# Attention and the experts' entry in one block: normalization, turns and gate logits of seven batches inside the attention's last steps

## What is computed

```python
# L0 attention: 16 heads of 64, relative bias
scores = einsum("bqhd,bkhd->bhqk", q, k) / 8 + bias
x = layernorm(x + softmax(scores) @ v @ Wo)
# L0 ffn: 8 experts, each token takes the best two, one after the other
gate_logits = x @ gate_W + gate_b
gate_weights = softmax(gate_logits)
topk_vals, topk_idx = top_k(gate_weights, 2)
out_1 = expert[idx_1](x);  out_2 = expert[idx_2](x + 0.5 * out_1)
x = layernorm(layer_norm(x + w_1 * out_1 + w_2 * out_2, gamma, beta))
```

## Time and profile before

| what | us |
|---|---|
| median of three runs | 1908.12 |
| the three runs | 1909.07, 1902.9, 1908.12 |
| the profiled execution | 1909.93 |
| its span, first to last instruction | 1907.8 |
| from the span's start to the end of the attention's last addition | 804.6 |
| from there to the gates' exponential | 26.4 |

### The profile page before, as it was taken

How to read it: one execution, slowest core, us unless ns; L and a number is a source line. 1 busy time by engine, 2 the same in 40 slices (tenths; PEclk the granted TensorE clock), 3 DMA queues, 4 the chain that set the end, 5 groups by cost and what they waited for, 6 DMA issues and landing times. The chain is left out here.

```text
span 1907.8 us, 39508 instructions
## 1 busy us (share of the span) xinstructions
PE 1648.2 (86%) x13660; PEld 1256.1 (66%) x13660; DVE 1381.2 (72%) x3837; ACT 1189.6 (62%) x2778; POOL 703.1 (37%) x667
## 2 busy tenths in 40 slices
PE   8999999999999999847685879999899989933871
PEld 6666666666666666536573458887688868822761
DVE  6888888888888888667566657776777755577324
ACT  6888888888888888546464656664556634511323
POOL 0222222222212122205457029994599921000772
PEclk9999999999999999978896889999999999955886
DMA  7000000000000000044652000000000000031544
GB/s 247 2 2 2 2 2 2 2 2 2 2 2 2 2 2 2 20 85 96 107 134 65 1 1 1 2 1 1 1 1 1 1 3 3 1 111 50 132 84 99
DMA packets 64007, 60.88 MB, mean 32 GB/s; under 512 B 10922, under 2 KB 53908, under 8 KB 63684
## 3 DMA queue, kind: packets, MB, share of 16 engines
q1 hardware_dynamic: 51348, 40.72, 7.0%
q0 software_dynamic: 10384, 16.59, 5.2%
q10 hardware_dynamic: 2080, 1.05, 0.2%
HBM read 39.60 MB, written 18.73 MB: 31 GB/s over the span
## 5 line engine op out<-in xcount | busy, mean ns | idle before, releaser
L377 ACT ACTIVATE prob<-prob,negmax 128x512 f32<-128x512 f32 x512 | 368.2, 721 | 51.9 <-DVE negmax L453 51.8
L167 POOL TENSOR_TENSOR x<-x,scaled 128x512 f32<-128x512 f32 x128 | 164.2, 1283 | 638.9 <-DVE scaled L474 629.7
L453 DVE CUSTOM_DVE_ANT_0 prob<-score_ps,bias 128x512 f32<-128x512 f32 x512 | 336.5, 685 | 4.9 <-issue 0.7
L276 PE MATMUL work_ps<-probT,val 128*64 128x512 f32 x1024 | 233.8, 598 | 0.1
L239 PE MATMUL score_ps<-k,q 64*128 64x512 f32 x1536 | 229.5, 415 | 3.3 <-DVE negmax L453 3.2
L461 DVE COPY probT<-turn_ps 128x512 f32<-128x512 f32 x256 | 176.1, 688 | 69.7 <-PE turn_ps L260 65.4
L260 PEld LDWEIGHTS turn_ps<-ident,prob 64*128 64x128 f32 x4096 | 162.7, 139 | 87.4 <-ACT prob L377 52.7
L362 ACT COPY probT<-turn_ps 128x512 f32<-128x512 f32 x256 | 148.7, 581 | 75.3 <-PE turn_ps L260 75.2
L260 PE MATMUL turn_ps<-ident,prob 64*128 64x64 f32 x4096 | 177.2, 225 | 3.1 <-DVE probT L461 1.8
L239 PEld LDWEIGHTS score_ps<-k,q 64*128 64x128 f32 x1536 | 134.4, 187 | 28.3 <-DVE k L437 2.5
L276 PEld LDWEIGHTS work_ps<-probT,val 128*64 128x64 f32 x1024 | 67.8, 136 | 114.2 <-issue 109.1
(11 more groups left out here) (513 smaller groups left out, 4105.6 us busy)
## 6 DMA issues: line engine op xcount, KB each, us to landing
ew<-L_ffn_fc_weight SPq DMA_DIRECT2D x32, 256.0 KB, 3.2
bias<-bias_line SPq DMA_DIRECT2D x16, 448.0 KB, 8.6
mid_rows<-row SPq DMA_DIRECT2D x40, 128.5 KB, 4.0
last_rows<-row SPq DMA_DIRECT2D x40, 64.0 KB
rows_dram<-qk SPq DMA_DIRECT2D x1, 2304.0 KB, 10.0
x_rows<-x SPq DMA_DIRECT2D x4, 512.0 KB, 7.2
acc_dram<-zero POOLq DMA_DIRECT2D x1, 2048.0 KB, 12.7
out<-x SPq DMA_DIRECT2D x4, 512.0 KB
```

Of the source, the lines that this page charges most:

```text
L167: pool.tensor_tensor(mine, mine, scaled[a][:, :, :], ALU.add).then_inc(added, 1)
L276: mm = pe.matmul(work[0][head(a), :], val[p // 2 % 2][:, c, p % 2 * 2 + a, :], probT[:, c, a, :], start=(c == 0), stop=(c == QT - 1))
L377: act.activation(mine, mine, ACT.Exp, bias=negmax[p % 2][:, i, a:a + 1], scale=-1.0, accum_out=total[p % 4][:, i, a:a + 1]).then_inc(exp_d ...
L453: dve.tensor_tensor_reduce(prob[p % 2][a][:, i, :], score_ps[i % 2][a][:, :], bias[:, h, first:first + SEQ][:, ::-1], -1.0, 3.0e38, ALU.ad ...
```

## The change

The entry is taken out, and its work goes into the attention's block. SOON is 28: tiles 0 to 27 are the seven batches whose attention is complete before the last step.

- The statistics of the 28 tiles are taken by DVE one at a time at the end of steps 10 to 61 (`look_in_step`), four to a batch.
- The last pair's turns use the two banks of turn_ps and of score_ps[0] in turn, so `turn(63, c)` waits for the copies of chunk c - 2 and not c - 1.
- In the tail, DVE forms the 28 tiles' moments; ACT loads the table of the square root, takes the root and normalizes 8 tiles, DVE 20. PE turns the tiles in groups of 8, 8, 8 and 4, as halves of 64 rows, two transposes to a tile, and forms the logits from halves too: each half has its own PSUM bank, and DVE adds the two. No idle transposes.
- The last pair's output is added to the last batch by DVE (8 instructions with a scale and an addition) and not by POOL; the batch's four tiles follow as a second group.
- SP stores 28 tiles of x to x_rows in three DMAs inside the block and waits for them at its end; the last four tiles, the experts' weights and the bias rows are issued in `gates_0`.
- The gates begin with the maximum, since the bias has been added. Their logits lie in a part of a wider tile (`shares`).
- `line` lies in the two tiles of `scaled`; it is stored by two DMAs.

```diff
+E_0, H_0 = 8, 256
+W1_W = H_0 + H_0 // P
+
+
+SOON = TILES - SEQ // P
+ROWS_OF = (range(0, 8), range(8, 16), range(16, 24), range(24, 28), range(28, 32))
+BY_ACT = tuple(t for t in range(SOON) if t < 16 and t % 8 < 4)
+BY_DVE = tuple(t for t in range(SOON) if t not in BY_ACT)
+LAST_BY_ACT, LAST_BY_DVE = (SOON, SOON + 1), (SOON + 2, SOON + 3)
...
-        table, line = core.sb(st, "table", [BUCKETS, HEADS]), core.sb(st, "line", [HEADS, 2 * SEQ])
+        table, line = core.sb(st, "table", [BUCKETS, HEADS]), [flat(scaled[c][0:HEADS, :, :]) for c in range(2)]
+        gw, gb, w = core.sb(st, "gw", [P, E_0]), core.sb(st, "gb", [P, E_0]), keep["shares"][:, :, 0:E_0]
+        norms = Norms(core, st, ends=[SOON, TILES])
...
+        logits_in = lambda banks, t: [banks[r][:, 0:t * E_0].rearrange("p (t e) -> p t e", t=t) for r in range(2)]
+        soon_ps, late_ps = logits_in(score_ps[1], SOON), logits_in(turn_ps, TILES - SOON)
+        logit_of = lambda r, t: soon_ps[r][:, t, :] if t < SOON else late_ps[r][:, t - SOON, :]
+        x_bank = lambda g, r: (turn_ps if g % 2 else score_ps[0])[r][:, 0:len(ROWS_OF[g]) * P // 2]
+        xT_all = [flat(prob[0][a][:, :, :]).rearrange("p (t r q) -> p t r q", r=2, q=P // 2) for a in range(2)]
+        xT_of = lambda t: xT_all[t // (TILES // 2)][:, t % (TILES // 2), :, :]
+        xT_group = lambda g, r: xT_all[ROWS_OF[g][0] // (TILES // 2)][:, ROWS_OF[g][0] % (TILES // 2):ROWS_OF[g][0] % (TILES // 2) + len(ROWS_OF[g]), r, :]
+        split = lambda bank: bank.rearrange("p (t q) -> p t q", q=P // 2)
...
-        of_bank = lambda r: turn_ps[r][:, :].rearrange("p (a t q) -> p a t q", a=2, t=QT)
+        of_bank = lambda p, c, r: (score_ps[0] if p == STEPS - 1 and c % 2 else turn_ps)[r][:, :].rearrange("p (a t q) -> p a t q", a=2, t=QT)
...
-            sp.dma_start(bias_line, line[:, :]).then_inc(line_out, 16)
-            sp.wait_ge(line_out, 16)
+            for c in range(2):
+                sp.dma_start(bias_line[:, c * SEQ:(c + 1) * SEQ], line[c]).then_inc(line_out, 16)
+            sp.wait_ge(line_out, 32)
...
+            sp.dma_start(gw[:, :], ins["L0_ffn_gate_W"]).then_inc(g_in, 16)
+            sp.dma_start(gb[:, :], ins["L0_ffn_gate_b"].partition_broadcast(P)).then_inc(g_in, 16)
+            to_rows = keep["x_rows"].rearrange("(t p) d -> p t d", p=P)
+            for n, (first, end) in enumerate(((0, 8), (8, 16), (16, SOON))):
+                sp.wait_ge(by_act, sum(t < end for t in BY_ACT))
+                sp.wait_ge(by_dve, sum(t < end for t in BY_DVE))
+                sp.dma_start(to_rows[:, first:end, 0:D], x[:, first:end, :]).then_inc(x_out, 16)
+            sp.wait_ge(g_in, 32)
+            sp.wait_ge(x_out, 48)
...
-            for p in range(STEPS):
+            for p in range(STEPS - 1):
...
+                    if p == STEPS - 1 and c >= 1:
+                        pe.wait_ge(turned_by_act, QT * p + c - 1)
+                        pe.wait_ge(turned_by_dve, QT * p + c - 1)
+                    elif p >= 1 or c >= 1:
...
+            def turn_normed(g):
+                mine = ROWS_OF[g]
+                if g < 4:
+                    pe.wait_ge(by_act, sum(t <= mine[-1] for t in BY_ACT))
+                    pe.wait_ge(by_dve, sum(t <= mine[-1] for t in BY_DVE))
+                else:
+                    pe.wait_ge(by_act, len(BY_ACT) + len(LAST_BY_ACT))
+                    pe.wait_ge(by_dve, len(BY_DVE) + len(LAST_BY_DVE))
+                if g < 2:
+                    pe.wait_ge(turned_by_act, QT * STEPS - g)
+                    pe.wait_ge(turned_by_dve, QT * STEPS - g)
+                else:
+                    pe.wait_ge(xT_by_act, g - 1)
+                for n, t in enumerate(mine):
+                    for r in range(2):
+                        mm = pe.transpose(split(x_bank(g, r))[:, n, :], x[half_of(r), t, :], ident[half_of(r), half_of(r)])
+                mm.then_inc(rows_turned, 1)
+
+            def logits(g):
+                pe.wait_ge(xT_by_act, g + 1)
+                if g == 4:
+                    pe.wait_ge(xT_by_dve, 1)
+                if g == 0:
+                    pe.wait_ge(g_in, 32)
+                for t in ROWS_OF[g]:
+                    for r in range(2):
+                        mm = pe.matmul(logit_of(r, t), xT_of(t)[half_of(r), :, :], gw[half_of(r), :], start=True, stop=True)
+                mm.then_inc(logits_done, 1)
...
+            for s in range(-1, STEPS):
                 step(s)
+            context(LAST - 1, 3)
+            turn(LAST, 0)
+            turn(LAST, 1)
+            turn(LAST, 2)
+            add_heads(LAST - 1)
+            turn(LAST, 3)
+            for c in range(QT):
+                context(LAST, c)
+            turn_normed(0)
+            add_heads(LAST)
+            turn_normed(1)
+            logits(0)
+            turn_normed(2)
+            logits(1)
+            turn_normed(3)
+            logits(2)
+            logits(3)
+            turn_normed(4)
+            logits(4)
...
+            for s in range(-2, LAST):
                 step(s)
                 if s == -2:
                     high_parts(4)
                     high_parts(5)
+            exps(LAST, 2, 0)
+            exps(LAST, 2, 1)
+            exps(LAST, 3, 0)
+            turn(LAST - 1, 3)
+            exps(LAST, 3, 1)
+            norms.warm_up(act)
+            turn(LAST, 0)
+            norms.root(act, 0)
+            copy_context(LAST - 1)
+            turn(LAST, 1)
+            turn(LAST, 2)
+            act.wait_ge(norms.shift_ready, 1)
+            normalize(BY_ACT[0])
+            turn(LAST, 3)
+            for t in BY_ACT[1:]:
+                normalize(t)
+            copy_context(LAST)
+            for g in range(4):
+                copy_normed(g)
+            norms.root(act, 1)
+            act.wait_ge(norms.shift_ready, 2)
+            for t in LAST_BY_ACT:
+                normalize(t)
+            act.wait_ge(rows_turned, 5)
+            act.copy(xT_group(4, 0), split(x_bank(4, 0))).then_inc(xT_by_act, 1)
...
+            def look(t):
+                dve.bn_stats(norms.raw[:, t, :], x[:, t, :]).then_inc(norms.seen, 1)
+
+            def look_in_step(s):
+                t = (s - PAIRS - 2) // PAIRS * QT + (s - PAIRS - 2) % PAIRS
+                if PAIRS + 2 <= s < STEPS - 2 and (s - PAIRS - 2) % PAIRS < QT:
+                    if t % QT == 0:
+                        dve.wait_ge(added, 2 * PAIRS * (t // QT + 1))
+                    look(t)
...
+            def bias_logits(of, logit_ps, n):
+                dve.wait_ge(logits_done, n)
+                dve.tensor_tensor(w[:, of, :], logit_ps[0][:, :, :], gb[:, :].unsqueeze(1).to_broadcast([P, of.stop - of.start, E_0]), ALU.add).then_inc(part_ready, 1)
+
+            def add_logits(of, logit_ps, n):
+                dve.wait_ge(part_ready, n)
+                dve.tensor_tensor(w[:, of, :], w[:, of, :], logit_ps[1][:, :, :], ALU.add)
...
+                look_in_step(s)
+            score(LAST, 2, 1)
+            turn(LAST - 1, 2)
+            scale_head(LAST - 2, 0)
+            score(LAST, 3, 0)
+            scale_head(LAST - 2, 1)
+            turn(LAST - 1, 3)
+            score(LAST, 3, 1)
+            for n in range(6):
+                norms.moments(dve, 0, n)
+            invert(LAST - 1)
+            turn(LAST, 0)
+            turn(LAST, 1)
+            norms.moments(dve, 0, 6)
+            norms.moments(dve, 0, 7)
+            turn(LAST, 2)
+            scale_head(LAST - 1, 0)
+            scale_head(LAST - 1, 1)
+            turn(LAST, 3)
+            invert(LAST)
+            dve.wait_ge(norms.shift_ready, 1)
+            for t in BY_DVE:
+                normalize(t)
+            dve.wait_ge(sum_done, STEPS)
+            dve.wait_ge(inv_ready, STEPS)
+            dve.wait_ge(added, 2 * LAST)
+            for a, summed in enumerate((summed_0, summed_1)):
+                for i in range(QT):
+                    t = SOON + i
+                    if a == 1:
+                        dve.wait_ge(summed_0, i + 1)
+                    dve.scalar_tensor_tensor(x[:, t, :], work[a][:, tile_of(i)], inv[LAST % 4][:, i, a:a + 1], x[:, t, :], ALU.mult, ALU.add).then_inc(summed, 1)
+            for i in range(QT):
+                dve.wait_ge(summed_1, i + 1)
+                look(SOON + i)
+            for n in range(6):
+                norms.moments(dve, 1, n)
+            dve.wait_ge(g_in, 32)
+            early, late = slice(0, SOON), slice(SOON, TILES)
+            norms.moments(dve, 1, 6)
+            norms.moments(dve, 1, 7)
+            dve.wait_ge(norms.shift_ready, 2)
+            for t in LAST_BY_DVE:
+                normalize(t)
+            bias_logits(early, soon_ps, 4)
+            dve.wait_ge(rows_turned, 5)
+            dve.tensor_copy(xT_group(4, 1), split(x_bank(4, 1))).then_inc(xT_by_dve, 1)
+            add_logits(early, soon_ps, 1)
+            bias_logits(late, late_ps, 5)
+            add_logits(late, late_ps, 2)
...
```

(14 more changed lines are left out.)

152 lines of the change are left out of this document (31 added, 121 removed).

## The result

The changed kernel took 1894.97 us (median of four runs, 1890.6 to 1895.42) against 1907.34 for the kernel before (median of four, 1902.9 to 1909.07): a ratio of 0.9929, interval 0.9917 to 0.9941. Measured again beside the first experiments, with six runs of it and 17 of the kernel before, it was 1894.69 against 1909.79: 0.9926, interval 0.9912 to 0.9939. That is 12.4 us in the first comparison and 15.1 in the second, and each interval spans some 5 us. The profiled execution took 1890.6 us for a span of 1888.9.

A forecast was written before the change was run, and what follows sets the result against it. TensorE was taken to bound the attention, followed by a 26.4 us chain of latencies. Moving the exponential from 830.99 to 813.3 gained 17.7 us, less 0.4 at the start: 17.3 net, median 1890.8, own range 1887 to 1894, wider 1886 to 1898.

The forecast's parts named there:

- The sum: Whole kernel: 17.7 us gained up to the gates' exponential, 0.4 lost at the start, 17.3 net; median 1890.8.
- Attention's steps, 0: Attention's steps: 28 statistics of 0.20 us each fit DVE's slack and cost 0; upper bound 5.7 us.
- Start, +0.4: Attention's start: the bias line's second DMA delays the bias loads, which the third pair's first score awaits; 0 to 0.5.
- Tail, −0.9: Attention's tail: with the second pair of banks, the last context starts at 794.7 and not 795.62; 0 to -1.8.
- the drain that the Trainium skill gives: Tail: 1.38 us behind a 1.28 table load; forecast took none, with it the forecast would be 1.4 us higher.
- Turns and logits, 0.061 a load: New PE block: 128 half-height logit loads at 0.061 take 7.8 us, 64 half transposes at 0.036 take 2.3.
- The clock: PE clock in the new block: stays 1.00 until the block's end; no fall in the sum.
- The rival: New block: the clock falls, slowing turns and logits from 800.7 by a factor of 1.7, +6.5 us, 1897.3; chance 0.15.
- The last rows: Block's end: DVE and ACT finish the last rows at 807.9, PE's 28 tiles' logits at 808.3; PE last by 0.4.
- The 0.5 put down for one copy: Block's end: one copy of 0.5 us stands between the last group's turn and its logits.
- The way out: Block's end to exponential: boundary 1.18 us, then 1.41 behind ACT's table load; bias addition's removal gains next to nothing, bias rows hidden.
- Behind the exponential: moved bodily: Stages behind the gates' exponential: same code, so they shift by whatever the exponential shifts.

The follow-up runs named there:

- e7: Kernel before with only the statistics added, one look in each of 28 DVE steps; ratio 1.0004 to the kernel before.
- e8: Kernel before with four statistics in each of the same 28 DVE steps; ratio 1.0066 to the kernel before.
- e1: Changed kernel again, unaltered, six runs; 1894.69 us, ratio 0.9926 to the kernel before.
- e2: Changed kernel with one full-height (128-row) idle transpose ahead of each of the first 28 tiles' half-height logits; ratio 1.0003 to the kernel before.
- e10: Changed kernel with the last turns ahead of the fourth group's logits and DVE's last copy ahead of its bias addition; 1888.89 us, ratio 0.9910 to the kernel before.
- e11: Changed kernel with full-height turns and logits, an idle transpose at every second tile, and both moves of e10; ratio 0.9934 to the kernel before.
- e9: Changed kernel with four half-height (64-row) idle transposes ahead of each of the first 28 tiles' logits; ratio 0.9922 to the kernel before.
- e5: Changed kernel with full-height turns and logits and one 128-row idle transpose ahead of each of the first 28 tiles' logits; ratio 0.9931 to the kernel before.
- e4: Changed kernel with turns and logits of the block over all 128 rows, no idle transposes; ratio 0.9930 to the kernel before.

## Why the prediction was right, step by step

**The sum.** Forecast 1890.8 with a range of 1886 to 1898; the medians measured were 1894.97 and 1894.69, 4 us higher. Forecast for the exponential: 813.3, with the start's 0.4 813.7; measured 815.17 and 816.0. So 17.3 us were expected up to there, and 15.8 and 15.0 came: 1.5 to 2.3 of the 4 us had been lost by then, for the most part by the clock (below). The rest isn't separated by these runs. It is no more than the medians of the unchanged kernel differ by from one comparison to the next (1906.92 to 1909.79, where the sum took 1908.1).

**Attention's steps, 0: right.** PE lost nothing, and the reason given, the room behind the look's place, was tested: e7 is no slower, and e8 puts the room at about 0.39 us.

**Start, +0.4: not seen.** The wait in the earlier trace rows is there, but its end differs by 0.7 us between the two profiles of the changed kernel itself (27.98 and 28.65). If the second issue costs anything, it is hidden in this.

**Tail, −0.9: right, and a little more came.** From the last exponential's end to the context 5.98 us before and 4.69 after, so −1.3. The context started at 794.69 where 794.7 was forecast and 795.1 with the start's 0.4. The warm-up at 791.32 stands 1.30 behind the load at 790.02, and the same 1.30 lie between 813.87 and 815.17. So the drain that the Trainium skill gives ("ScalarE: Activation LUTs", section "What ACT_TABLE_LOAD costs") did not show here either.

**Turns and logits, 0.061 a load: right at full clock.** In a pure group 32 loads took 1.88, 0.059 each, and 16 half transposes 0.58:
```profile
800.46 1.88 PEld L376 LDWEIGHTS score_ps<-gw,prob 64*128 64x128 f32 x32
```

**The clock: the term that was wrong.** The forecast had it at 1.00 to the block's end, put nothing for a fall into the sum, and gave the rival 0.15. It fell in every kernel with narrow logits and no idle work. The rival's mechanism came, at less than its price: it was priced from 800.7 on at +6.5, and the fall came at 806.0 (804.6 in e1), when two thirds (in e1 half) of the logits and all but the last turns were done. The forecast gave no reason for a later fall, and between 803.7 and 806.5 the place is luck, since it went with the beginning of the attention's fast stretch. The rival's factor of 1.7 was a little low: from one group's start to the next, 48 loads took 5.09 us behind the fall in e1 (0.106 each) and 32 took 1.76 at full clock (0.055), a factor of 1.9. Measured: 48 logits 4.17 for 2.9, 16 logits 1.88 for 0.97, the turn 0.68 for 0.45, together +2.4. The terms before the fall were 0.6 too high in sum: the logits of tile 16 and on began at 804.84, where the forecast's own terms give 805.4. That leaves the 1.8 us by which the block's end, 812.47, is later than the 810.7 forecast. The step that failed is the weighing: 11.3 us at 1.00 with idle transposes between the earlier trace rows were taken as evidence against a fall, beside the remark that the change takes these away. The remark was the stronger half: without idle work the clock never lasted, though e2 shows that idle work alone is no safeguard.

**The last rows: right, but not the wait behind them.** PE was the last, as forecast, by more than forecast, since the fall slowed it: the rows were ready at 807.4 and PE reached them at 808.85. The 0.5 put down for one copy was 0.61. With both moves of e10 it is hidden.

**The way out: right.** The boundary took 1.16 us (1.18 forecast). The exponential stands 1.30 behind the start of ACT's table load (1.41 before), and the load began 0.24 behind DVE's first instruction, so 1.5 us where 1.41 were taken. DVE waits 1.18 for ACT there: dropping the addition of the bias gained next to nothing, as forecast. The bias rows come late, and hide behind the exponential with nothing lost:
```profile
815.74 0.60 PE L824 MATMUL b_ps<-ident,b_rows 16*128 16x16 f32 x2 [3.72 <-DMA b_rows<-L_ffn_b]
```

**Behind the exponential: moved bodily: right.** In the second comparison the total gained what the exponential gained (15.1 and 15.0), in the first it gained 12.4 for 15.8. The single profile shows 3.1 more than the exponential's shift, and 2.7 of that lies in one unchanged stage with another granted clock. So "moved bodily" holds to within some 3 us, and no better is shown.

## What to carry to other kernels

Where two stages of pure latency follow a long stage with one full engine, put their work into the other engines' slack in it; measure that slack by adding the work to the old kernel once and then four times over, which here gave about 0.39 us a step. When a stage's idle work on TensorE is removed together with the waits that it filled, put a fall of the clock into the sum and not only among the rivals, from the size of the work behind it (here it cost 2.4 us, where a fall at the first logits was priced at 6.5). To compare two variants of a block, take the time from its own start and note where in it the clock fell: the place of the exponential alone would have given e10 up to 1.5 us, where 0.75 are its own. A gain found at one place should be compared over many runs with the shift of that place: the first pair of profiles here showed 3 us that the repeat didn't bear out.

## What was unexpected of the hardware

- TensorE's granted clock fell to 0.50 at 803.7 to 806.5, amid matmuls of 8 columns and turns of x that kept the engine busy without a gap, in all six kernels without idle work (seven profiles). With idle transposes of 64 or 128 columns between them it fell at 806.5 (e2), 807.9 (e11), 810.6 (e9) and 814.9 (e5). What decides it is open.
- In nine of the fourteen profiles the attention's fast stretch lasted 774.8 us, whatever stood at its end: an engine idle for 4 us (before), narrow matmuls without a gap (changed kernel), or the same with idle transposes of full height (e2).
- Instructions of 64 and of 128 rows in turn cost more than their sum at full clock: 0.58 us a tile in e2 against 0.24 + 0.12 for its two parts alone; in e9 and e5, of one height, a tile with its idle work was 0.35 and 0.285.
- Half-height fp32 loads in alternating halves take 0.059 us, full-height ones 0.117 (16 in 1.87 us, e4). A tile has four of the one or two of the other, so both forms cost 0.235 a tile, and splitting the rows brings nothing to the logits; it does to the turns (0.66 against 1.09 for eight tiles).
- The same code of the projection took from 24.2 to 27.4 us; the granted clock in its first 8 us was 1.00 in the seven profiles with 24.2 to 24.7, 0.79 or 0.80 in the six with 26.1 to 26.2, and 0.59 in the one with 27.4.
